# Four buffers instead of two for the rows of three mixture-of-experts layers, loops written out by four, and a last combine that adds on VectorE

## The reference

```python
x = x + _L0_gnn_ref(_layernorm(x, axis=-1), adj, ...)
x = x + _L0_ffn_ref(_layernorm(x, axis=-1), ...)   # 16 experts, hidden 256, gated, top 2
x = x + _L1_gnn_ref(...)
x = x + _L1_ffn_ref(...)                           # 8 experts, hidden 512, top 1, a capacity
x = x + _L2_gnn_ref(...)
x = x + _L2_ffn_ref(...)
x = x + _L3_gnn_ref(...)
x = x + _L3_ffn_ref(...)                           # attention, then 8 experts, hidden 341, gated, top 2
```

## Time and profile before

| what | value |
|---|---|
| median of 3 runs | 3395.41 us (3390.82 to 3404.48) |
| the profiled execution | 3369.56 us |
| its span, first to last instruction | 3367.8 us |
| PE / DVE / ACT / POOL busy share of the span | 81% / 65% / 52% / 26% |
| granted TensorE clock, mean | 0.912 |
| experts of ffn0, from PE's first to its last transposes | 568.9 to 857.9 us |
| experts of ffn1, the same | 1141.7 to 1298.5 us |
| experts of ffn3, the same | 2971.9 to 3283.1 us |
| last combine | from about 3314 us to the end |

### The profile page before, as it was taken

How to read it: one execution, slowest core, us unless ns; L and a number is a source line. 1 busy time by engine, 2 the same in 40 slices (tenths; PEclk the granted TensorE clock), 3 DMA queues, 4 the chain that set the end, 5 groups by cost and what they waited for, 6 DMA issues and landing times. The chain is left out here.

```text
span 3367.8 us, 68105 instructions
## 1 busy us (share of the span) xinstructions
PE 2731.9 (81%) x19770; PEld 2142.4 (64%) x19770; DVE 2195.4 (65%) x6539; ACT 1751.4 (52%) x5050; POOL 872.8 (26%) x863
## 2 busy tenths in 40 slices
PE   5799995787777686578999997899978777569995
PEld 4566674777467575366787776566655445468883
DVE  5666674444567554668888885799986677544443
ACT  2233332444466353465656563677757666445554
POOL 0222333444425333330010001000001434434331
PEclk9899997989878798889999999899999888689998
DMA  5111111222332111320000000000010000022125
GB/s 194 43 51 43 57 45 50 63 63 63 125 123 74 50 51 54 135 66 1 1 0 0 0 1 22 14 25 19 25 59 8 25 20 21 27 57 56 53 55 162
DMA packets 142570, 168.85 MB, mean 50 GB/s; under 512 B 19920, under 2 KB 118224, under 8 KB 141776
## 3 DMA queue, kind: packets, MB, share of 16 engines
q1 hardware_dynamic: 116688, 118.67, 11.9%
q0 software_dynamic: 21504, 44.74, 3.9%
q10 hardware_dynamic: 4224, 3.59, 0.4%
HBM read 115.87 MB, written 51.05 MB: 50 GB/s over the span
## 5 line engine op out<-in xcount | busy, mean ns | idle before, releaser
L1363 PE MATMUL bank<-ffn_e_xT,ffn_e_mine 128*128 128x128 f32 x3360 | 454.7, 284 | 27.3 <-ACT ffn_e_mine L1297 11.7
L1221 POOL DMA_INDIRECT y_rows<-ffn_e_rows_out,ffn_e_scatter_at x352 | 339.1, 963 | 522.4 <-DVE ffn_e_rows_out L1249 331.1
L1363 PEld LDWEIGHTS bank<-ffn_e_xT,ffn_e_mine 128*128 128x128 f32 x3360 | 421.8, 199 | 35.4 <-issue 30.0
L744 POOL DMA_INDIRECT sorted_rows<-ffn_rows,ffn_slot x320 | 315.9, 987 | 229.7 <-issue 218.3
L1269 DVE TENSOR_TENSOR ffn_e_hid<-ffn_e_act,bank 128x256 f32<-128x256 f32 (+1 forms) x280 | 135.9, 485 | 274.1 <-ACT ffn_e_act L1323 214.8
L1373 PE MATMUL bank<-ffn_e_mine,ffn_e_hid 128*128 128x128 f32 x1968 | 292.0, 283 | 9.0 <-issue 5.0
L1297 ACT ACTIVATE ffn_e_mine<-constants 128x512 f32 (+1 forms) x352 | 250.4, 712 | 93.3 <-issue 80.6
L1373 PEld LDWEIGHTS bank<-ffn_e_mine,ffn_e_hid 128*128 128x128 f32 x1968 | 258.1, 197 | 15.3 <-issue 6.6
L2736 ACT ACTIVATE gnn_prob<-bank,gnn_low 128x256 f32<-128x256 f32 x512 | 203.1, 500 | 108.0 <-DVE gnn_low L2650 108.0
L1323 ACT ACTIVATE ffn_e_act<-bank 128x256 f32<-128x256 f32 (+1 forms) x280 | 120.5, 430 | 244.1 <-PE bank L1363 199.3
L1257 DVE TENSOR_SCALAR ffn_e_mine<-constants 128x256 f32 (+2 forms) x352 | 124.0, 354 | 131.1 <-PE bank L1373 68.1
(11 more groups left out here) (514 smaller groups left out, 6558.3 us busy)
## 6 DMA issues: line engine op xcount, KB each, us to landing
g_adj<-in_adjT SPq DMA_DIRECT2D x48, 512.0 KB, 3.8
ffn_e_rows_in<-sorted_rows SPq DMA_DIRECT2D x346, 66.0 KB
ffn_c_y<-y_rows SPq DMA_DIRECT2D x80, 256.0 KB, 3.1
g_adj_rows<-in_adj SPq DMA_DIRECT2D x16, 512.0 KB
gnn_adj<-in_adjT SPq DMA_DIRECT2D x16, 512.0 KB, 3.9
constants<-in_ffn SPq DMA_DIRECT2D x1, 6281.0 KB, 23.0
y_rows<-ffn_e_rows_out,ffn_e_scatter_at POOLq DMA_INDIRECT x352
constants<-in_ffn SPq DMA_DIRECT2D x1, 5204.0 KB, 15.4
```

What stands on the lines that cost most here:

```text
L744: eng.indirect_dma_start(c.sorted_rows, bass.IndirectOffsetOnAxis(r.slot[par][:, k, j:j + 1], 0), r.rows[par][:, j, :], None).then_inc(r.d ...
L1221: g.indirect_dma_start(c.y_rows, bass.IndirectOffsetOnAxis(scatter_at[par][:, k:k + 1], 0), rows_out[par][:, k, :], None).then_inc(scatter ...
L1363: ins = pe.matmul(chunk(part, ch), chunk(weights[:, i * HALF:(i + 1) * HALF], ch), x, start=True, stop=True)
```

## The change

1. `ROUTE_DEPTH` is 4 in all three layers: `r.rows` and `r.slot` have four buffers, and DVE's wait in `vector_shift` is for the scatter of four turns ago.
2. `rows_in` has four buffers with a semaphore each: SP's wait is for quad q-4 instead of q-2. PE and DVE take buffer q mod 4.
3. Loops that touch these buffers are written out by four: `by_fours` in gnn0 and in the experts of all three layers, `staggered_fours` in att3. The last argument of `STAGES` stays, its third goes from 6 to 8, so that att3's loop has one iteration of four turns.
4. In the last combine PE's and ACT's part is gone; DVE adds the sum to X. SP waits for that alone.

```diff
+def staggered_fours(eng, body, ahead, behind, begin, left):
+
+    for t in range(-ahead, begin):
+        body(t, t % 4)
+    with eng.Fori(begin, TURNS - left - 3, 4) as t:
+        for i in range(4):
+            body(t + i, i)
+    for t in range(TURNS - left, TURNS + behind):
+        body(t, t % 4)
+
+def by_fours(eng, body, count=TURNS):
+
+    stop = 4 + 4 * ((count - 5) // 4)
+    for t in range(4):
+        body(t, t, t == 0, False)
+    with eng.Fori(4, stop - 3, 4) as t:
+        for i in range(4):
+            body(t + i, i, False, False)
+    for t in range(stop, count):
+        body(t, t % 4, False, t == count - 1)
...
-ROUTE_DEPTH = {"ffn0": 2, "ffn1": 4, "ffn3": 2}
+ROUTE_DEPTH = {"ffn0": 4, "ffn1": 4, "ffn3": 4}
...
-        rows_in = [sb(f"rows_in{i}", [P, Q, ROW]) for i in range(2)]
+        rows_in = [sb(f"rows_in{i}", [P, Q, ROW]) for i in range(4)]
...
-                    wait_past(sp, xT_ps, q - 1)
-                    wait_past(sp, token_ready, q - 1)
+                    wait_past(sp, xT_ps, q - 3)
+                    wait_past(sp, token_ready, q - 3)
                     for k, at in zip(mine, places):
-                        sp.dma_start(rows_in[par][:, k, :], c.sorted_rows[ds(at, P), :]).then_inc(gathered[par], 16)
-                every_turn(sp, load, QUADS)
+                        sp.dma_start(rows_in[four][:, k, :], c.sorted_rows[ds(at, P), :]).then_inc(gathered[four], 16)
+                by_fours(sp, load, QUADS)
...
                     if t >= DEEP:
-                        sp.wait_ge(added_ps, t - DEEP + 1)
+                        sp.wait_ge(rows_ready if ends else added_ps, t - DEEP + 1)
                         if ends:
-                            sp.wait_ge(rows_ready, t - DEEP + 1)
                             store(t - DEEP)
...
                         ins.then_inc(summed, 1)
+                        if ends:
+                            v.wait_ge(summed, t + 1)
+                            rows_ = c.X[:, ds(t * TT, TT), :]
+                            v.tensor_tensor(rows_, rows_, acc[:], ALU.add).then_inc(rows_ready, 1)
...
-                for t in range(TURNS):
+                for t in range(0 if ends else TURNS):
                     par, bank = t % DEEP, B[t % 8][:]
...
-                    if t >= 2:
+                    if t >= 2 and not ends:
                         rows_out(t - 2)
-                rows_out(TURNS - 2)
-                rows_out(TURNS - 1)
+                for t in range(TURNS if ends else TURNS - 2, TURNS):
+                    rows_out(t)
...
-    STAGES = (2, 3, 6, 4)
+    STAGES = (2, 3, 8, 4)
```

More of the change, by code:

```diff
@@ L334, in _, with turn @@
                 route.pool_begin(g)
-                def turn(t, par, first, last):
+                def turn(t, four, first, last):
+                    par, one, two = four % 2, (four + 3) % 4, (four + 2) % 4
                     if first:
@@ L448, in turn @@
                     if not first:
-                        route.vector_shift(v, t - 1, 1 - par, before)
+                        route.vector_shift(v, t - 1, one, before)
                     if not last:
@@ L465, in turn @@
                     if not first:
-                        route.vector_first(v, t - 1, 1 - par, before)
+                        route.vector_first(v, t - 1, one, before)
                         route.vector_second(v, t - 1, before)
@@ L1200, in _, with load @@
             def _(sp):
-                def load(q, par, first, last):
+                def load(q, four, first, last):
                     mine = range(Q // 2) if first else range(Q)
@@ L1258, in copy_second, with quad @@
                                     ALU.mult).then_inc(second_copied, 1)
-                def quad(q, par, first, last):
+                def quad(q, four, first, last):
                     experts = quad_experts(v, q)
@@ L1331, in quad, with to_features @@
                             evac_xT(q + 1, 1 - par)
-                every_turn(a, quad, QUADS)
+                by_fours(a, lambda q, four, first, last: quad(q, four % 2, first, last), QUADS)
             @block.tensor
             def _(pe):
-                def to_features(q, par):
-                    pe.wait_ge(gathered[par], 8 * Q * (q - par) + 16 * Q)
+                def to_features(q, four):
+                    pe.wait_ge(gathered[four], 4 * Q * (q - four) + 16 * Q)
                     wait_past(pe, xT_ready, q)
                     for k in range(Q):
-                        ins = pe.transpose(B[0][:, k * P:(k + 1) * P], rows_in[par][:, k, 0:D], c.ident[:])
+                        ins = pe.transpose(B[0][:, k * P:(k + 1) * P], rows_in[four][:, k, 0:D], c.ident[:])
                     ins.then_inc(xT_ps, 1)
@@ L1376, in _, with quad @@
                 to_features(0, 0)
-                def quad(q, par, first, last):
+                def quad(q, four, first, last):
+                    par = four % 2
                     for k in range(Q):
@@ L2986, in with_x1, with turn @@
                     g.tensor_tensor(c.X[:, rows_, :], c.X[:, rows_, :], c.X1[:, rows_, :], ALU.add)
-                def turn(t, par):
+                def turn(t, four):
+                    par = four % 2
                     if on(t - 1):
@@ L3208, in turn @@
                         evac_T(1, 1)
-                staggered(a, turn, *STAGES)
+                staggered_fours(a, turn, *STAGES)
             @block.tensor
```

70 lines of the change are left out of this document (35 added, 35 removed).

## The result

The changed kernel took 3379.73 us (median of 5 runs, 3373.91 to 3387.16), the kernel before, beside it, 3398.17 us (5 runs). The ratio is 0.9948, 95% interval 0.993 to 0.9967: 18 us less, just past the 0.5% that this measurement can tell. The forecast was 3312 us, 83 less, with a range from 3290 to 3350. The direction held, the size is off by more than a factor of four, and the time lies 30 us above the range.

What follows compares the result with a forecast made beforehand. PE was taken to bound the experts steps, losing time to late rows in ffn0 and ffn1. Terms -61 (ffn0), -15 (ffn1), 0, 0, -7 (combine) sum to -83 us: 3286.6 against the profiled 3369.56, scaled to 3312; range 3290 to 3350.

Steps and rivals of the forecast that it cites:

- 35 x (8.24 - 6.5) = 61: ffn0: with rows in time, 35 quad intervals shrink from 8.24 to 6.5 us, gaining 61 us.
- Both ways to the 6.5: ffn0's quad without waits: 6.33 us from one interval less its wait, 6.63 from ffn3's time per record; 6.5 taken.
- ffn1: Experts step ffn1: four row buffers remove most of PE's later waits for rows, gaining 15 us, bounds 5 and 19.
- ffn3: Experts step ffn3: gains nothing, because its rows are there in time; PE is busy 287 of 312 us.
- The router's buffers and loops: Four router buffers and loops by four: put at 0 us, the loops with bounds -2 to +3.
- slower: Rival, 0.03: each of 15 jumps back fetches code again, two packets of 1.4 us each, 42 us if all hit PE.
- The comparison with gnn3: Loops: gnn3's long iterations run without an instruction packet on PE, so gnn0's 1202 records should still fit.
- The combine: Last combine: quicker turns, earlier first store and shorter end together save 7 us, bounds 3 and 10.
- the pace of 2.6: Last combine: DMA engines bind, so turns come every 2.6 us; eleven turns save 0.33 us each, 3.7 us.
- It does little: Rival, 0.04: PE would have waited for something else right behind the late rows; time within 0.5%.
- the ring: Rival, 0.12: PE, ACT, DVE set ffn0's pace, 7.2 us a quad; -46, 3349 us. Signs: PE waits L1297/L1269, SP still waits.
- SP bound: Rival, 0.15: SP's loads become ffn0's bound at 7.3 us a quad, gaining 43 instead of 61; total -65, 3330 us.

Runs made afterwards that it cites:

- e7: The kernel before with the change to the last combine alone; 0.9973 of the kernel before on chip A.
- e6: The changed kernel with gnn0, att3 and the routers' depth as in the kernel before; 0.9951 of the kernel before on chip A.
- e2: The kernel before with the experts' scatters replaced by plain stores, rows not at their tokens' places; 0.9522 of the kernel before on chip A.
- e13: The kernel before itself, run again unchanged on chip C for a trace; one run, 3098.17 us.
- e15: The changed kernel with gnn0, att3 and the routers' depth as in the kernel before, on chip C; 0.9924 of the kernel before.
- e4: The changed kernel with ACT and DVE keeping loaded expert numbers in the written-out four quads; 0.9914 of the kernel before on chip A.
- e11: The changed kernel with scatters spaced one to each PE unit, expert numbers kept, gnn0 and att3 as before; 0.9917 of the kernel before on chip B.
- e9: The changed kernel itself, run again on chip B; 0.994 of the kernel before.
- e17: The changed kernel with scatters spaced one to each PE unit, expert numbers kept, gnn0 and att3 as before; 0.9667 of the kernel before on chip D.
- e1: The changed kernel with the experts' scatters replaced by plain stores, rows not at their tokens' places; 0.952 of the kernel before on chip A.
- e3: The changed kernel with the second, third and fourth scatter of a quad each waiting for a unit of a later quad; 0.9868 of the kernel before, chip A.
- e5: The changed kernel with only the third scatter of a quad waiting, so scatters go two and two; 0.9862 of the kernel before on chip A.
- e14: The changed kernel itself, run again on chip C; 0.9951 of the kernel before.

## Why the prediction was wrong

**The step that failed** is the price of a quad without late rows in ffn0, "35 x (8.24 - 6.5) = 61". By the traces ffn0's 35 intervals gained 7 us on the first chip (8.24 to 8.04 a quad), 12 on chip A (286.4 in e7 to 274.6 in e6) and 12.6 on C, which has no holes (6.17 to 5.81 a quad). The premise under it was that PE's wait for rows is added to all else. It wasn't. In the kernel before, the scatters at 706.80 to 711.56 are followed by a pause of 2.4 us of ACT and DVE from 709.36 on, and PE's wait of 3.07 us for rows ends at 713.63:

```profile
709.36 0.29 DVE L1257 TENSOR_SCALAR ffn_e_mine<-constants 128x256 f32 x1
...
711.78 0.38 ACT L1323 ACTIVATE ffn_e_act<-bank 128x256 f32<-128x256 f32 x1 [2.57 <-PE bank L1363]
712.20 0.42 DVE L1269 TENSOR_TENSOR ffn_e_hid<-ffn_e_act,bank 128x256 f32<-128x256 f32 x1 [2.54 <-issue]
```

The rows were late in microseconds that overlap those in which the others were held, and partly from the same cause: in e2, without the scatters, PE's wait for rows is 17.6 us instead of 65.8, still with two buffers. Taking the wait away left the hold.

**The check that should have caught it** failed as well. Both ways to the 6.5 (6.33 from one interval less its wait, 6.63 from ffn3) used stretches with scatters in them. They agreed with each other and so looked like PE's own need, which is 5.80. The prediction's rows had a sign as well: from 713.63 to 721.11 in the earlier trace rows a quad takes 7.48 us though the rows of the next are there in time. And the third interval of the kernel before, ahead of its first scatter at 587.2, is 6.0 us, those behind it 7.4, 9.2 and 9.3.

**ffn1**, priced at 15, gave nothing that shows: the late rows are gone, and jumps that wait for code take some 7 us in it. Without these it gained 4 us on chip A (e7 to e6) and 1 on C (e13 to e15). **ffn3** gained nothing, as said, but not because PE was full: some 35 of its 312 us were holes, too.

**The router's buffers and loops**, put at 0 with a bound of +3, cost 8 us on chip C (0.27%, where the two intervals do not overlap). The mechanism is that of the rival "slower", at 2.7 to 3.8 us a jump instead of 1.4 a packet, but in three jumps of fifteen and on DVE, not on PE. The comparison with gnn3 looked only at PE's window, where the trace indeed shows nothing.

**The combine**, 7 us, measured 8.8 by itself (e7) and 10.7 to 11.6 in the traces. The DMA engines were not full at 268 GB/s: they move 300 at a turn of 2.18 us, so the pace of 2.6 was too high and the term 2 to 5 us too small.

**The rivals.** "It does little" (0.04) is nearest to what happened, with the reason that was given for it. The one with 0.12, the ring, has one of its two signs, waits for L1324 and L1296 in place of rows, but not the other, SP still waiting; register loads are worth some 11 us in ffn0 on chip A (e4) and nothing that shows on B (e11, 201.7, against 203.6 in e9). Its 7.2 us a quad was too short, since it left the holes out. "SP bound" (0.15) shows at most in e17, where a quad takes 7.0 us on average. The term that no case had is the hold behind four scatters.

**What is shown and what is not.** Shown: the experts' holes and 160 us go when their scatters become plain stores (e1, e2); they are there on A, D and the chip of the first comparison and absent on B and C, for the same programs; four in a row costs ffn3 35 us, three and one or two and two don't (e3, e5). Not shown: what in the chip is held, and why only on some. Nor is it shown what about a scatter does it: a plain store of the same 64 KB (some 32 packets a DMA in either form) also goes to rows in order and takes POOL 0.54 us instead of 0.96. What is held is not PE alone, in any case. SP's register instructions in ffn0 in the changed kernel (first fence, a chip with holes) and in e14 (second):

```profile
L1215 SPq TENSOR_LOAD <-ffn_offsets x111: 3/267/728, 619.7 to 841.1; - x111
L1215 SPq SEQ_ASSERT  x111: 5/18/722, 620.5 to 841.9; - x111
```
```profile
L1215 SPq TENSOR_LOAD <-ffn_offsets x120: 261/266/438, 545.4 to 710.5; - x120
L1215 SPq SEQ_ASSERT  x120: 18/18/18, 545.9 to 711.0; - x120
```

An instruction that always takes 18 ns in this stage on the one chip takes up to 722 on the other.

## What to carry to other kernels

A wait in the profile is worth what the next constraint leaves of it. Before pricing it, find the engine's own rhythm in a stretch without the suspected neighbours (here: the interval of 5.80 us ahead of the first scatter) and ask whether the wait and another engine's pause have one cause. Measure a small gain on more than one chip. And a loop written out further can cost in another stage: look behind every jump back, on every engine, for a gap with instruction packets.

The best version for both sorts of chip keeps the experts' four buffers and the combine, leaves gnn0 and att3 alone, keeps the loaded expert numbers and spaces the scatters: 0.9917 of the kernel before on B, 0.9667 on D. On a chip without holes the last two items bring nothing that can be told: without them it is 0.9924 on C (e15).

## What the runs showed of the hardware

- Chips differ in one respect by 9% of this kernel: 3352 to 3404 us against 3096 to 3107 for the kernel before. Nearly all of it lies where POOL issues indirect DMAs, though not in gnn1, whose 64 cost no more; 1210 us without any agree to within 0.1 us.
- Four indirect DMAs of 128 rows, each 0.96 us on POOL and 1.26 apart, are followed on the former chips by pauses of mostly 2 to 3.6 us of ACT and DVE, eight in a row (att3) by pauses of up to 6.5 us. The same bytes by plain DMAs, 0.54 us each on POOL, are not.
- A DVE loop of 293 instructions jumps back in 0.3 us (e15) or in 3.6 (e14); the two kernels differ only in other stages.
